# Rotary queries: the swapped halves come from a VectorE shuffle instead of a second TensorE product

## The reference, cut to what matters

```python
def _apply_rope(t, cos, sin):
    t1, t2 = jnp.split(t, 2, axis=-1)
    rot = jnp.concatenate([-t2, t1], axis=-1)
    return t * cos[None, :, None, :] + rot * sin[None, :, None, :]
...
h = _rmsnorm(x, ln1_w)
qkv = jnp.einsum('bsh,oh->bso', h, wqkv)
q = qkv[..., :NH * HD].reshape(B, S, NH, HD)
...
q = _apply_rope(q, cos, sin)
```

## Time and profile before

| what | value |
|---|---|
| time, median of 3 runs | 1434.44 us (1430.58 to 1437.1) |
| span of the profiled execution, first to last instruction | 1431.4 us |
| TensorE busy (matmuls) | 1298.2 us, 91% |
| VectorE busy | 775.3 us, 54% |
| ScalarE busy | 730.7 us, 51% |
| GpSimd busy | 531.9 us, 37% |
| mean granted TensorE clock | 0.984 |

### The profile page before, as it was taken

One profiled execution on the slowest core, in us unless ns is written; L12 is line 12 of the kernel. 1 busy time (PEld: TensorE's weight loads), 2 busy tenths in 40 slices (PEclk: granted clock), 3 DMA queues, 4 the chain that ended last, 5 costly groups with the idle time before them and its releaser, 6 DMA issues. The chain is left out here.

```text
span 1431.4 us, 25003 instructions
## 1 busy us (share of the span) xinstructions
PE 1298.2 (91%) x9332; PEld 1059.5 (74%) x9332; DVE 775.3 (54%) x1791; ACT 730.7 (51%) x1297; POOL 531.9 (37%) x745
## 2 busy tenths in 40 slices
PE   9899999988999999996778999898889888999995
PEld 7576776757999999995455656656556656999995
DVE  4886868774111111112665697986877554543432
ACT  6464756552322222221366777777867656434341
POOL 2113040402000000004798887877868123322222
PEclk9999999999999999998999999999999999999998
DMA  9674462901877777832100011010011605322221
GB/s 354 264 191 121 115 181 77 259 19 59 314 262 262 264 267 267 319 107 83 41 1 4 11 39 34 1 42 16 12 42 40 250 33 181 61 43 49 40 44 12
DMA packets 71272, 171.14 MB, mean 120 GB/s; under 512 B 8572, under 2 KB 47489, under 8 KB 61168
## 3 DMA queue, kind: packets, MB, share of 16 engines
q1 hardware_dynamic: 55520, 144.39, 31.1%
q0 software_dynamic: 10224, 16.09, 4.9%
q10 hardware_dynamic: 5408, 9.04, 1.7%
HBM read 123.11 MB, written 48.07 MB: 120 GB/s over the span
## 5 line engine op out<-in xcount | busy, mean ns | idle before, releaser
L1200 ACT ACTIVATE b_ht<-ps,b_b 128x154 f32<-128x154 f32 x256 | 85.3, 387 | 203.9 <-PE ps L1167 188.1
L2354 POOL DMA_INDIRECT experts<-ye,gidx_all x32 | 32.4, 1012 | 323.2 <-SPq L1106 312.7
L1215 DVE TENSOR_SCALAR b_yt<-ps,b_b 128x154 f32<-128x154 f32 x64 | 21.2, 374 | 241.0 <-PE ps L1180 241.0
L1167 PE MATMUL ps<-b_xet,ring 128*128 128x154 f32 x1024 | 141.1, 295 | 3.3 <-ACT b_ht L1200 3.3
L1180 PE MATMUL ps<-b_ht,ring 128*128 128x154 f32 x1024 | 139.7, 294 | 0.4 <-DVE b_yt L1215 0.4
L1167 PEld LDWEIGHTS ps<-b_xet,ring 128*128 128x128 f32 x1024 | 135.7, 189 | 3.4 <-issue 3.4
L1180 PEld LDWEIGHTS ps<-b_ht,ring 128*128 128x128 f32 x1024 | 136.2, 189 | 0.6 <-issue 0.6
L2638 POOL DMA_INDIRECT out_dram<-d_yd,d_to x39 | 60.8, 1558 | 149.3 <-DVE d_yd L2606 120.4
L1537 DVE TENSOR_REDUCE c_mx<-ps 128x8 f32<-128x1024 f32 x64 | 77.8, 1215 | 58.2 <-PE ps L1481 57.8
L2587 DVE TENSOR_TENSOR d_g<-d_gs,ps 128x512 f32<-128x512 f32 x37 | 25.4, 688 | 124.1 <-PE ps L2524 124.1
L1500 PE MATMUL ps<-cf,experts 128*128 128x128 f32 x512 | 68.7, 278 | 12.6 <-ACT experts L1570 6.5
(11 more groups left out here) (343 smaller groups left out, 2981.1 us busy)
## 6 DMA issues: line engine op xcount, KB each, us to landing
ring<-in_w SPq DMA_DIRECT2D x64, 1024.0 KB, 5.3
xd<-zero SPq DMA_DIRECT2D x6, 3120.0 KB
a_kp<-in_ctx_k SPq DMA_DIRECT2D x8, 1024.0 KB
d_xd<-xd SPq DMA_DIRECT2D x39, 130.0 KB, 2.1
xe<-zero SPq DMA_DIRECT2D x1, 4928.0 KB, 37.0
b_xe<-xe SPq DMA_DIRECT2D x32, 154.0 KB
ye<-b_ye ACTq DMA_DIRECT2D x32, 154.0 KB
experts<-in_wd SPq DMA_DIRECT2D x1, 4608.0 KB
```

What stands on the lines that cost most here:

```text
L1167: r = pe.matmul(ps[:, b, CAP * (m % 2):CAP * (m % 2) + CAP], w1r[:, slot, k, P * m:P * m + P], xet[:, e % 2, k, :], start=(k == 0), stop=( ...
L1200: r = a.activation(ht[:, e % 2, m, :], ps[:, b, CAP * (m % 2):CAP * (m % 2) + CAP], ACT.Gelu, bias=b1[:, e, m:m + 1])
```

## The change

The second query product (rq1) and its swapped weights are left out. In its place VectorE swaps the two halves of each head by one `stream_shuffle`, which permutes the partitions within each group of 32 by the list `HALVES`, from the PSUM bank into a new SBUF tile `other`. The product with the sines and the addition then work on `other`. Four VectorE instructions now stand in the piece rq0r, and the piece rqr is gone. rv waits for the end of the cosine product (`rq_read`), which follows the shuffle on the same engine, instead of for the final sum.

```diff
+HALVES = [(i + HD // 2) % HD + i // HD * HD for i in range(32)]
...
-        self.wa, self.wc, self.wf = region.take(4, KD, D), region.take(3, KD, D), region.take(3, KD, D)
+        self.wa, self.wc, self.wf = region.take(4, KD, D), region.take(3, KD, D), region.take(2, KD, D)
...
+        other = sb("other", [P, 2 * GS, P])
...
-            for half in range(2):
-                yield at("rq%d" % half)
-                if half == 0:
-                    pe.wait_ge(*two.k_in.at(g))
-                else:
-                    pe.wait_ge(*rq_half.at(g))
-                by_channel(c, MIX, w.wf[:, half, :, :], rot.xt).then_inc(*rq.up())
+            yield at("rq0")
+            pe.wait_ge(*two.k_in.at(g))
+            by_channel(c, MIX, w.wf[:, 0, :, :], rot.xt).then_inc(*rq.up())
             yield at("rv")
-            pe.wait_ge(*two.q_in.at(g))
+            pe.wait_ge(*rq_read.at(g))
             by_token(c, MIX, w.wv, rot.xt).then_inc(*rv.up())
...
             yield at("rq0r")
-            v.wait_ge(*rq.at(g, 0))
+            v.wait_ge(*rq.at(g))
+            v.stream_shuffle(in_=ps[:, MIX, :], out=other[:, :, :].rearrange("p n l -> p (n l)"), mask=HALVES).then_inc(*c.dv.up())
+            turned = c.dv.now()
             if g:
                 v.wait_ge(*two.sc.at(g - 1))
-            v.tensor_tensor(units(two.qt), bank, wide(0), ALU.mult).then_inc(*rq_half.up())
-            yield at("rqr")
-            v.wait_ge(*rq.at(g, 1))
-            v.wait_ge(*kr_in.at(g))
-            v.tensor_tensor(bank, bank, wide(1), ALU.mult).then_inc(*c.dv.up())
+            v.tensor_tensor(units(two.qt), bank, wide(0), ALU.mult).then_inc(*rq_read.up())
+            v.wait_ge(*turned)
+            v.tensor_tensor(other[:, :, :], other[:, :, :], wide(1), ALU.mult).then_inc(*c.dv.up())
+            v.wait_ge(*rq_read.at(g))
             v.wait_ge(*c.dv.now())
-            v.tensor_tensor(units(two.qt), units(two.qt), bank, ALU.add).then_inc(*two.q_in.up())
+            v.tensor_tensor(units(two.qt), units(two.qt), other[:, :, :], ALU.add).then_inc(*two.q_in.up())
...
-    a["wf"] = stack([q.T, q[swap].T, x["L1_ffn_wo"].T])
+    a["wf"] = stack([q.T, x["L1_ffn_wo"].T])
```

More of the change, by code:

```diff
@@ L1642, in phase_c @@
             s(x) for x in ("xk", "xki", "xv", "xvi", "xq", "xqi", "xs", "xdi", "xei", "xtr", "xpi", "xo"))
-        rk, kr_in, rr, rq, rq_half, rv = s("rk"), s("kr"), s("rr"), s("rq", 2), s("rqh"), s("rv")
+        rk, kr_in, rr, rq, rq_read, rv = s("rk"), s("kr"), s("rr"), s("rq"), s("rqread"), s("rv")
         meta, x3, sq, root2, rows_in, lg_mm, lg_in = s("meta"), s("x3"), s("sq"), s("root2"), s("rows"), s("lgm"), s("lgi")
@@ L2078, in last_tensor @@
             pe.wait_ge(*last.xt_in.at(2 * g))
-            by_token(c, TOP, w.wf[:, 2, :, :], last.xt).then_inc(*oj2.up())
+            by_token(c, TOP, w.wf[:, 1, :, :], last.xt).then_inc(*oj2.up())
             yield at("t6")
```

## The result

The kernel with the change takes 1459.45 us (median of 4 runs, 1458.29 to 1466.76), beside 1435.77 us for the kernel before on the same chip (1430.58 to 1441.72). The ratio is 1.0176, with a 95% interval of 1.0149 to 1.0204: it is slower, by 24 us. The span of the profiled execution is 1457.7 us, 26.3 more than before, and the mean granted clock is 0.973 where it was 0.984.

The account below looks back on a forecast made before the run. No engine alone was the bound; ordered hand-overs between engines were. Losses of 18.1 us, the removed product's 15 us inside, less 4.5 absorbed, left 13.5: span 1431.4 to 1445, plus 3.0, gives 1448 us, range 1434 to 1462.

Parts of the forecast that it names:

- What bounds the kernel: In phase_c no engine alone is the bound; the ordered piece that ends last at each hand-over decides.
- The removed product: Eight TensorE matmuls per pair go: 1.85 us per pair, 15 us over 8 pairs, 16.5 with a removed wait.
- The rival that TensorE wins: TensorE is the bound in phase_c and gains: 1418 us, or about 1424 with half the slack; chance 0.14.
- The shuffle: The added VectorE instruction in each pair, taken at 0.70 us.
- The wait of the earlier trace: TensorE's wait for L2023 ahead of the second query product goes: 1.7 us in two places.
- The lock: VectorE's sine product and addition, now reading two SBUF tiles, and GpSimd instructions exclude each other; losses 18.1 us with it.
- one of its signs: In the profile after, L2025 and L2028 on VectorE would have medians well over 0.69 us.
- the engines take turns: VectorE's two-tile instructions and GpSimd's pieces alternate, the second to come standing still until the first ends.
- Pair by pair: Losses in pairs 0 to 6 of 1.1, 4.1, 3.9, 1.1, 3.4, 4.7 and 0.6 us; pair 7 wins 0.8.
- TensorE's busy time would be 15 us lower: Sign in the profile after: TensorE's busy time in phase_c 15 us lower, its idle time about 28 us higher.
- what is given back: A late TensorE finds results already there, so a quarter of the losses, 4.5 us, is absorbed.
- The prediction without the lock: Rival that the lock is absent or seldom meets: losses 5.2 us less a quarter, 1438 us; chance 0.22.

Follow-up runs that it names:

- e_keep: The kernel with the change, with a second query product still computed on TensorE at its old place and read by nobody; 1458.82 us, ratio 1.0181.
- e_split_noshuf: The kernel before with its second query product taken out and nothing put in its place (halves not swapped); 1428.31 us, ratio 0.9962.
- e_turn_warm: e_turn plus 11 query products that nobody reads, in TensorE's long waits of pairs 1, 2, 4, 5 and 6; 1452.01 us, ratio 1.0114.
- e_turn: The kernel with the change, plus one wait that holds a GpSimd multiplication until VectorE's expert choice is done; 1460.61 us, ratio 1.0168.
- e_psum: The kernel with the change, but the shuffle works in place in PSUM and the value product waits for the addition; 1448.23 us, ratio 1.0105.
- e_noshuf: e_psum without the shuffle, three VectorE instructions in one piece, halves not swapped; 1434.2 us, ratio 1.0004.
- e_lock_one: The kernel before, with the sine product written to an SBUF tile so that the addition reads two SBUF tiles; 1441.43 us, ratio 1.0024.

## Why the prediction was right and where it was wrong

The direction was right, and 1459.45 lies in the range, but the forecast of 1448 is 11 us short: 13.5 us were forecast, 24 measured.

- **What bounds the kernel.** Right. No engine is alone the bound: 15 us of TensorE work brought nothing in the sum (e_keep) or 6.0 at best (e_split_noshuf).
- **The removed product.** The rival that TensorE wins fell: 1418 to 1424 was not reached even with nothing put in its place (1428.31).
- **The shuffle.** 0.735 us, taken at 0.70: right. The wait of the earlier trace rows went, as forecast.
- **The lock.** Right as a mechanism, and shown apart (one of its signs failed: L2028 was to have a median well over 0.69 us, and has 0.692, being held in three pairs only): 11.2 and 12.1 us between the versions with and without a second SBUF operand. The prediction had 18.1 with and 5.2 without, 12.9. That the engines take turns held in pairs 2 and 4; in pair 5 VectorE was held through both of GpSimd's pieces, which by chance costs the same (L1513 starts 6.75 us after its cosine product, against 6.8 by the forecast's 1083.3 and 1076.5).
- **Pair by pair.** The places are right, and the sizes are right in the sum where the clock stays up: in e_turn_warm pairs 1 to 6 lose 3.2, 3.5, 2.0, 4.4, 4.5 and 1.2 us, 18.8 in all, where 17.8 were forecast. In the kernel after the same pairs lose 29.3.
- **The failed step, the granted clock.** The sum priced a wait at its length. It has no term for what the wait does to TensorE's clock, although the windows of the kernel before had an example, ahead of the first changed pair:

```profile
775.00:780.00 5.00, 1.94 (x8) 1.57 (x8) 4.21 (x10) 1.28 (x2) 4.53 (x10) 0.71 0.00 0
780.00:785.00 5.00, 4.14 (x27) 1.81 (x28) 0.67 (x3) 3.90 (x7) 4.77 (x5) 0.61 0.00 0
```

Filling the waits gives 8.6 us back. Pair 6 shows it at its plainest: 0.6 forecast, 4.1 in the trace, 1.2 with the wait filled. That TensorE's busy time would be 15 us lower was wrong for the same reason: the half clock filled it up again.
- **The second failed step, "what is given back".** A quarter of the losses, 4.5 us, was taken as absorbed, with no row behind it. In pairs 1 to 6 nothing was: they lose at least what was forecast, in e_turn_warm (18.8 against 17.8) too. Something does come back behind pair 7's cosine product, 3.3 us in the kernel after and 4.3 in e_turn_warm (0.7 of it is the shuffle, which now stands ahead of that product), where 0.8 was forecast, and 1.7 of it is the clock behind the transfer, which nobody had priced. With 18.1 in place of 13.5, and 8.6 for the clock, the sum is 1461.1, and 1459.45 was measured. That it comes so near is partly luck, since neither what comes back at the end nor the lateness of pair 0 is in it.
- **A stall that nobody priced.** The lock also held the expert choice, which the change does not touch. Pair 2 is 3.7 us shorter without it, but taking it away (e_turn) did not shorten the kernel; in its trace pair 4 is 2.3 us longer beside a longer half clock, and the rest was not found.
- **The place alone.** The prediction without the lock had 5.2 us, less a quarter; e_psum, which is that kernel but for its later value product, has 12.5. So this term was too small by more than the lock's was. The difference is mainly in pairs 2 and 6, where e_psum loses 7.1 and 3.7 against 0.1 and 0.6 forecast. In pair 2, 4.5 us stand beside the half clock of the rows above; the other 2.6 are there in e_noshuf too, where the clock is up behind L1513, and both kernels have TensorE waiting 2.40 us for the choice of experts in that pair. In pair 6, where the clock was 0.50 from 1140 to 1145 us, it was not tried in this kernel, and stays argued.

## What to carry to other kernels

Before an operand is moved from PSUM to SBUF, look for GpSimd's long pieces beside that instruction: with two SBUF operands VectorE stands until they end, and a shuffle done in place in PSUM avoids it. Work taken off an engine that waits at that place is worth little, and what is put ahead of an instruction that other engines wait for can cost more than its length, or less: the shuffle, 5.6 us in all, cost 14.0 us in one order and 1.8 in another. Price a wait of TensorE with the clock behind it, by reading the clock and the durations of the groups that follow the longest waits of the kernel before, and treat it as something that may or may not happen: waits of 2.4 us had it in one pair here and not in two others. And when two kernels differ by 2 us, look whether they already differ at a place where their code is the same.

## What the runs showed of the hardware

- VectorE instructions of 128x512 with two SBUF operands took up to 4.77 us beside GpSimd's pieces in the kernel after (up to 2.43 in e_lock_one, with nothing else changed), those with one operand in PSUM 0.70 at most in all pairs. Instructions on 128x8 and 128x64 elements were held as well: 1.69 and 2.32 us instead of 0.17 and 0.23.
- After waits of 5.26 and 6.28 us (pairs 2 and 5 of the kernel after) the granted clock fell to 0.50 and a matmul group took 1.08 us instead of 0.64, in e_turn another 3.54 instead of 1.99. After one of 4.66 us (pair 4) the next group still took 0.64, and the clock was at 0.50 from 1040 to 1042.5 us. In e_psum it fell beside waits of 2.02 and 2.42 us (pairs 2 and 6), but not after those of 2.42 and 2.37 us in pairs 4 and 5. With matmuls read by nobody in the waits its mean from 850 to 1180 us was 0.99 instead of 0.94, and the kernel was 8.6 us faster with 20 us more work.
- Behind the expert transfer at the end of `phase_c` the clock was 0.66 over 5 us in four kernels' profiled executions and 1.00 in the other ten, for which the same two groups took 7.2 and 5.6 us.
- A shuffle of 128x512 within 32 partitions takes 0.72 to 0.75 us from PSUM to SBUF and 0.69 in place in PSUM.
- A VectorE instruction held by GpSimd is not always let in between two of GpSimd's pieces: 4.77 us through two of them in pair 5, and 4.81 in e_turn_warm.
- GpSimd's own piece grew from 2.37 to 2.79 us while two held instructions took their turns around it (pair 2).
